# Scores of a linear-attention kernel as three f32r products of key and query halves instead of one fp32 product

## The reference

```
qkv = silu(x @ w_qkv.T)                     # q, k, v: 16 heads of 128
for each block of tokens:
    o_inter = (q * q_decay) @ kv
    qk      = (q @ k.T) * diag_decay        # the scores
    o_intra = qk @ v
    kv      = block_decay * kv + (k * k_decay).T @ v
    out     = o_inter + o_intra
out = norm_w * out * rsqrt(mean(out^2) + eps)
y   = (sigmoid(x @ w_gate.T) * out) @ w_out.T
```

## Time and profile before

| what | value |
|---|---|
| median of 3 runs | 1790.89 us (1789.92 to 1792.35) |
| the profiled execution | 1791.69 us |
| its span, first to last instruction | 1788.9 us |
| granted TensorE clock over the span | 0.998 |
| busy: PE, PEld, DVE, ACT, POOL | 98%, 87%, 69%, 40%, 33% |

### The profile page before, as it was taken

One profiled execution on the slowest core, in us unless ns is written; L12 is line 12 of the kernel. 1 busy time (PEld: TensorE's weight loads), 2 busy tenths in 40 slices (PEclk: granted clock), 3 DMA queues, 4 the chain that ended last, 5 costly groups with the idle time before them and its releaser, 6 DMA issues.

```text
span 1788.9 us, 34315 instructions
## 1 busy us (share of the span) xinstructions
PE 1751.8 (98%) x12213; PEld 1565.2 (87%) x12213; DVE 1228.4 (69%) x2463; ACT 709.8 (40%) x1331; POOL 585.8 (33%) x794
## 2 busy tenths in 40 slices
PE   6999999999999999999999999999999999999998
PEld 5888899999888888888888888889999999999997
DVE  7888777777566665666656666667777777766566
ACT  4333333343444444444444444443434343333332
POOL 2222254544434333433334333323232323200011
PEclk9999999999999999999999999999999999999999
DMA  6665431322367676676766766623222222210013
GB/s 216 220 222 210 139 110 62 108 86 83 106 196 225 199 220 204 205 215 201 215 210 203 218 201 207 210 71 95 63 83 71 72 72 71 74 46 1 1 60 106
DMA packets 194872, 249.37 MB, mean 139 GB/s; under 512 B 27280, under 2 KB 161936, under 8 KB 194704
## 3 DMA queue, kind: packets, MB, share of 16 engines
q1 hardware_dynamic: 150032, 138.09, 26.0%
q0 software_dynamic: 32256, 83.93, 14.4%
q10 hardware_dynamic: 12416, 25.17, 3.8%
HBM read 135.92 MB, written 111.17 MB: 138 GB/s over the span
## 4 chain that ended last, share of the span: by engine, by line
PE 93%; DVE 4%; issue 2%; ACT 1%; DMA 1%; SPq 0%; POOL 0%; DVEq 0%; ACTq 0%; POOLq 0%
PE bank L1166 7%; PE bank L1146 7%; PE bank L1168 7%; PE bank L1167 7%; PE bank L1148 7%; PE bank L1147 7%; PE bank L1190 6%; PE bank L1207 6%; PE bank L1198 6%; PE bank L1210 6%; PE bank L1230 5%; PE bank L1238 3%; PE bank L1219 3%; PE bank L1221 3%; PE bank L1220 3%; PE bank L1183 3%
## 5 line engine op out<-in xcount | busy, mean ns | idle before, releaser
L520 POOL DMA_DIRECT2D xsT<-rows_turned x384 | 209.9, 553 | 331.8 <-PE bank L1230 188.9
L1166 PE MATMUL bank<-wh,xh 128*128 128x256 f32 x1024 | 311.0, 304 | 0.0
L614 ACT ACTIVATE kv<-bank 128x512 f32<-128x512 f32 x256 | 152.9, 597 | 342.2 <-PE bank L1168 342.2
L1168 PE MATMUL bank<-wh,xl 128*128 128x256 f32 x1024 | 288.6, 282 | 0.0
L1167 PE MATMUL bank<-wl,xh 128*128 128x256 f32 x1024 | 288.2, 281 | 0.0
L529 POOL DMA_INDIRECT yk<-slot_y,pos x128 | 127.5, 996 | 278.1 <-DVE xr L930 229.8
L958 DVE SCALAR_TENSOR_TENSOR state<-state,hc,bank 128x128 f32<-128x128 f32 x448 | 155.8, 348 | 85.0 <-PE bank L1198 71.4
L1166 PEld LDWEIGHTS bank<-wh,xh 128*128 128x128 f32 x1024 | 193.8, 189 | 15.9 <-issue 15.9
L1146 PE MATMUL bank<-xh,wh 128*128 128x512 f32 x512 | 207.2, 405 | 0.0
L1148 PE MATMUL bank<-xh,wl 128*128 128x512 f32 x512 | 202.4, 395 | 0.0
L1147 PE MATMUL bank<-xl,wh 128*128 128x512 f32 x512 | 201.9, 394 | 0.0
(11 more groups left out here) (162 smaller groups left out, 3637.6 us busy)
## 6 DMA issues: line engine op xcount, KB each, us to landing
slot_x<-zeros ACTq DMA_DIRECT2D x8, 3072.0 KB, 9.9
we<-wexp_in SPq DMA_DIRECT2D x192, 128.0 KB, 2.4
xs<-slot_x SPq DMA_DIRECT2D x96, 256.0 KB, 3.7
rows_turned<-xz POOLq DMA_DIRECT2D x96, 256.0 KB, 2.8
xsT<-rows_turned POOLq DMA_DIRECT2D x384, 64.0 KB, 2.7
slot_y<-ys SPq DMA_DIRECT2D x96, 256.0 KB, 2.7
wd<-wdown_in SPq DMA_DIRECT2D x192, 64.0 KB, 2.5
raw<-wqkv_in SPq DMA_DIRECT2D x16, 384.0 KB, 4.0
```

The costliest lines, as they stand in the source:

```text
L520: pool.dma_start(xsT[q % 2][b * TB:(b + 1) * TB, :, :, :].rearrange("p a k j -> p a (k j)"), xz_back[q % 2, b]).then_inc(xsT_loaded[q % 2] ...
L614: act.activation(kv[i % 2][:, 2 * half:2 * half + 2, :].rearrange("p c n -> p (c n)"), bank[half][:], ACT.Silu).then_inc((k_silu, v_silu)[ ...
L1166: pe.matmul(dst, lh, rh, start=(k == 0), stop=False)
L1168: mm = pe.matmul(dst, ll, rh, start=False, stop=(k == KD - 1))
```

## The change

Keys and queries are split in halves before the scores. ACT writes the transposed keys from bank 2 to `kTh` (f32r) instead of to `kT`, and DVE subtracts them from bank 2 to `kTl`. ACT copies qT to `qTh` (f32r), and DVE subtracts to `qTl`. `scores` makes three f32r products per chunk in place of one fp32 product. qT stays, for decay_queries. `qTl` takes the memory of `sm`; low_queries writes it after attend has read sm.

On TensorE `project_kv(s, 1)` follows `project_kv(s, 0)`, and `keys_values` and then `gate_up` stand next; `scores` has moved behind `project_out(s - 2, 0)`. On DVE `low_keys` is the first instruction of a slot, `update_state` and `gated(q0)` stand ahead of `decay_scores`, and `low_queries` stands between `add_out(.., 1)` and `low_og`. On ACT `high_q` follows `silu_q`.

```diff
@@ -174,10 +174,14 @@
         wos = keep("wos", [P, D])
         hc0 = keep("hc0", [P, TAB])
         kv = [keep(f"kv{i}", [P, CH, 2 * HD]) for i in range(2)]
-        kT = keep("kT", [P, SB])
+        kTh = keep("kTh", [P, SB], F32R)
+        kTl = keep("kTl", [P, SB], F32R)
         qT = keep("qT", [P, SB])
+        qTh = keep("qTh", [P, SB], F32R)
         qp = [keep(f"qp{i}", [P, SB]) for i in range(2)]
         kp = keep("kp", [P, SB])
+        with ExitStack() as st:
+            qTl = sb_in(st)("qTl", [P, SB], F32R)
         sm = keep("sm", [P, SB])
         tg = keep("tg", [P, SB])
         o2 = keep("o2", [P, SB])
@@ -259,7 +263,10 @@
         k_silu = sem("k_silu")
         v_silu = sem("v_silu")
         q_silu = sem("q_silu")
-        kT_ready = sem("kT_ready")
+        kTh_ready = sem("kTh_ready")
+        kTl_ready = sem("kTl_ready")
+        qTh_ready = sem("qTh_ready")
+        qTl_ready = sem("qTl_ready")
         tanh_done = sem("tanh_done")
         o2_ready = sem("o2_ready")
         ogh_ready = sem("ogh_ready")
@@ -620,6 +627,10 @@
                 act.wait_ge(s_mm, i)
                 act.activation(qT[:], bank[0][:], ACT.Silu).then_inc(q_silu, 1)
 
+            def high_q(i):
+                act.wait_ge(q_silu, i + 1)
+                act.copy(qTh[:], qT[:]).then_inc(qTh_ready, 1)
+
             def tanh_g(i):
                 act.wait_ge(g_mm, i + 1)
                 act.wait_ge(og_ready, i)
@@ -627,7 +638,7 @@
 
             def copy_kT(i):
                 act.wait_ge(kT_mm, i + 1)
-                act.copy(kT[:], bank[2][:]).then_inc(kT_ready, 1)
+                act.copy(kTh[:], bank[2][:]).then_inc(kTh_ready, 1)
 
             def square_o(j):
                 act.wait_ge(o_mm, j + 1)
@@ -673,6 +684,7 @@
                     result(q0)
                 if projects:
                     silu_q(s)
+                    high_q(s)
                 if attends:
                     square_o(s - 1)
                 if experts:
@@ -939,6 +951,14 @@
                     dve.wait_ge(ssq_added, d - NSB + 1)
                     dve.tensor_tensor(q, q, o2[:], ALU.add).then_inc(ssq_added, 1)
 
+            def low_keys(j):
+                dve.wait_ge(kTh_ready, j + 1)
+                dve.tensor_tensor(kTl[:], bank[2][:], kTh[:].bitcast(F32), ALU.subtract).then_inc(kTl_ready, 1)
+
+            def low_queries(i):
+                dve.wait_ge(qTh_ready, i + 1)
+                dve.tensor_tensor(qTl[:], qT[:], qTh[:].bitcast(F32), ALU.subtract).then_inc(qTl_ready, 1)
+
             def decay_scores(j):
                 dve.wait_ge(s_mm, j + 1)
                 dve.tensor_tensor(chunks(sm[:]), chunks(bank[2][:]), per_chunk(hc[j // NSB % 2][:, 0:P]),
@@ -1017,6 +1037,8 @@
                 projects, attends, delivers = s < NSTEP, 1 <= s <= NSTEP, 2 <= s <= NSTEP + 1
                 if s == 2:
                     first_phase_stored(dve)
+                if attends:
+                    low_keys(s - 1)
                 if delivers:
                     add_squares(s - 2)
                 if EXPERT0 <= s + 1 < EXPERT1:
@@ -1028,14 +1050,14 @@
                     weights()
                 if s in COMBINE:
                     combine(COMBINE.index(s))
-                if attends:
-                    decay_scores(s - 1)
-                if experts:
-                    gated(q0)
                 if s == 1:
                     dve.wait_ge(tab_stored, 16)
                 if attends:
                     update_state(s - 1)
+                if experts:
+                    gated(q0)
+                if attends:
+                    decay_scores(s - 1)
                 if projects:
                     decay_keys(s)
                 if EXPERT0 <= s + 1 < EXPERT1:
@@ -1052,6 +1074,8 @@
                     gated(q0 + 1)
                 if delivers:
                     add_out(s - 2, 1)
+                if projects:
+                    low_queries(s)
                 if attends:
                     low_og(s - 1)
                 if s == 0:
@@ -1185,9 +1209,12 @@
 
             def scores(j):
                 pe.wait_ge(q_silu, j + 1)
-                pe.wait_ge(kT_ready, j + 1)
+                pe.wait_ge(kTl_ready, j + 1)
+                pe.wait_ge(qTl_ready, j + 1)
                 for c in range(CH):
-                    mm = pe.matmul(bank[2][:, ch[c]], kT[:, ch[c]], qT[:, ch[c]], start=True, stop=True)
+                    pe.matmul(bank[2][:, ch[c]], kTh[:, ch[c]], qTh[:, ch[c]], start=True, stop=False)
+                    pe.matmul(bank[2][:, ch[c]], kTh[:, ch[c]], qTl[:, ch[c]], start=False, stop=False)
+                    mm = pe.matmul(bank[2][:, ch[c]], kTl[:, ch[c]], qTh[:, ch[c]], start=False, stop=True)
                 mm.then_inc(s_mm, 1)
 
             def keys_values(j):
@@ -1274,22 +1301,21 @@
                 projects, attends, delivers = s < NSTEP, 1 <= s <= NSTEP, 2 <= s <= NSTEP + 1
                 if projects:
                     project_kv(s, 0)
-                if attends:
-                    scores(s - 1)
+                    project_kv(s, 1)
                 if s > FIRST_OUT + 2:
                     turn_back(s - FIRST_OUT - 3)
-                if projects:
-                    project_kv(s, 1)
-                if experts:
-                    gate_up(q0)
                 if s == 0:
                     total_counts()
                 if s == 5:
                     expert_table()
                 if attends:
                     keys_values(s - 1)
+                if experts:
+                    gate_up(q0)
                 if delivers:
                     project_out(s - 2, 0)
+                if attends:
+                    scores(s - 1)
                 if experts:
                     down(q0)
                 if projects:
```

## The result

The changed kernel took 1846.9 us (median of 4 runs, 1844.5 to 1848.8), the kernel before 1790.7 (1789.9 to 1792.4): 1.0311 times as long, 95% interval 1.0295 to 1.0326, so 53 to 58 us more. Forecast: 1853 (1835 to 1891), slower.

A forecast was written before the change was run, and what follows sets the result against it. TensorE, busy 98% of the span, was taken as the bound: 1791.7 us + 60 for the score products + 3 for late DVE = 1855, less 0.8 for the median and 1 for a removed passage, gives 1853 (1835 to 1891).

The forecast's parts named there:

- The bound: TensorE, busy 98% of the span: a slot's time is the sum of its start-to-start times, 128 times over.
- The price of a narrow f32r product: In scores, each 128-column f32r product costs about its weight load, 0.114 us; twelve add 0.47 us a slot, +60 us.
- DVE late: In 3 routing slots and partly in a few others, decay_scores slips past its due time: 3 us for all.
- the case that was worked out: Slots also carrying routing and split_low_in: DVE is fuller, so decay_scores slips about 0.5 to 1.2 us past due.
- The time line of a combine slot: From first project_kv: scores 4.5 to 5.85 us, decay_scores 6.05 to 6.75, attend due at 7.25, margin 0.5 us.
- The rival of late scores: Unseen DVE or ACT latency makes attend wait; 0.3 us beyond the margin gives +38 us, 1891; chance 0.08.
- the first rival: In scores, a narrow f32r product streams at its columns, 0.065 us: -15 us, 1776; chance 0.10.
- the second rival: In scores, each narrow f32r product costs a whole fp32 product, 0.223 us: +228 us, 2018; chance 0.10.
- the removed passage: On TensorE, one passage between product kinds less a slot: saves up to 0.01 us a slot, 1 us.

The follow-up runs named there:

- the splits alone: Changed kernel with all halves made and waited for, but one fp32 product per chunk: 1796.6 us beside 1790.7 for the kernel before.
- one product: Changed kernel with only the high-by-high f32r product per chunk, both low terms left out: 1759.5 us.
- bf16 halves: Changed kernel with all four halves in bf16 instead of f32r, same twelve products: ratios 1.0043, 1.0041 and 1.0062 to the kernel before.

## Why the prediction was right

- *The bound.* TensorE's start-to-start sum set each slot: busy time +53.5, span +53.9.
- *The price of a narrow f32r product.* The step on which all hung: 0.11 us from the load rows. Measured 0.112, and shown to be the load by the runs with half the columns (1.343 us a stretch) and half the weights (0.774). I took 0.114, which was 0.02 us a slot or 3 us too much; the 0.112 of the load would have been the whole answer. Beside it: the rule of the Trainium skill, TensorE: Matmul & The Clock Gate, section on weight-path perf modes, which the prediction weighed, is that fast weight load is on with 128 weights and an input type that isn't FP32. The traces agree for bf16 (load record 98 ns, 0.056 us a product) and not for f32r (192 ns, 0.112), if f32r counts as not FP32.
- *128 times 0.45 is 57.6 us; the trace has 53.9.* What the sum lacked: in the 48 expert slots the growth is 0.40 and not 0.45, 2.4 us less. There scores is followed by down, the products of 64 rows, and a stretch of scores costs 0.397 more than with fp32 (1.271 us against 0.874 in the run with the splits alone). Slot 26, where TensorE had stood 2.1 us in front of project_out, is 1.7 us shorter instead of 0.45 longer, and slot 25 0.4 us shorter, 3.0 us less together. The first phase, which the change leaves alone, came out 1.1 us shorter (191.4 against 192.5). With the 2.3 us of the next point these make 53.4.
- *DVE late.* 3 us forecast; beyond the common 0.45, slots 1, 2, 4 and 20 grew by 1.4, 0.1, 0.2 and 0.6, 2.3 us. (With the splits alone slots 1 to 24 lost 5.3, which fits DVE having less time in a slot that isn't longer.) Slot 20 is the case that was worked out, routing and split_low_in together; DVE's timeline in it, then TensorE's:

```profile
420.00 1.22 DVE L843 TENSOR_TENSOR wl<-raw,wh 128x1024 fp32r<-128x1024 f32 x1
421.14 1.11 DVE L978 SCALAR_TENSOR_TENSOR state<-state,hc,bank 128x128 f32<-128x128 f32 x3
422.16 0.68 DVE L964 TENSOR_TENSOR sm<-bank,hc 128x512 f32<-128x512 f32 x1
```

```profile
422.90 0.49 PE L1234 MATMUL bank<-sm,kv 128*128 128x128 f32 x2 [0.31 <-DVE sm L964]
```

- *The time line of a combine slot.* decay_scores was put at 6.05 to 6.75 with a margin of 0.5 before attend. In a combine slot of the changed kernel, on DVE:

```profile
1257.10 1.49 DVE L978 SCALAR_TENSOR_TENSOR state<-state,hc,bank 128x128 f32<-128x128 f32 x4
1258.99 0.69 DVE L964 TENSOR_TENSOR sm<-bank,hc 128x512 f32<-128x512 f32 x1 [0.40 <-PE bank L1217]
```

This slot began at 1252.98, so decay_scores ran from 6.01 to 6.70, and attend started at 1260.24, which is 7.26, against 7.25 in the prediction: a margin of 0.56. update_state ended before scores did, and DVE waited 0.40 us for scores. The rival of late scores needs a shorter slot than this one: with scores at 0.45 us (one product) or 0.75 (bf16) DVE's lateness does show.
- *Nothing faster, nothing at fp32's price.* The 0.065 us of the first rival is what bf16 halves get, and better (0.056); f32r products with 128 weight columns that follow one another are 0.11 apart. The 0.223 us of the second rival no f32r product takes.
- ACT and the removed passage: ACT right (busy 43%, 42 forecast). The passage of 0.01 us a slot can't be told from the rest.

## What to carry to other kernels

Count weight loads, not columns, when the moving side is narrow. Here an fp32 product of 128 columns was two records with a load of 0.11 us each, and the three f32r products that replace it have one record each but also one such load each. So they take 0.34 us where the fp32 product took 0.22.

Where one engine is busy 98% of the span, look for the rows in which it has the least else to do, here loads before products of one column, or just after a stall. They price the term that the usual rows hide.

## What the runs showed that I had not expected

- The first two products behind a 512-column one start 0.06 us apart, then 0.11: the first one's load had run behind those columns and cost nothing. With half the weight columns or with bf16 all products are 0.060 and 0.056 us apart.
- Halving the weight columns shortened the load record by 57 ns (192 to 135), about what it took off the spacing (52).
- On three of the chips the kernel before was 94 to 102 us slower and the mean clock of a run 0.97 to 0.98 instead of 1.00. The traces from there show stops in eight routing slots, and handovers from TensorE to ACT up to 2.6 us long, the late ones all beside GpSimd's indirect DMAs. On the chips of 1790.7 us the same DMAs don't delay that handover. Why the chips differ stays open.
